# Three bank pairs for the gram products, and the inverse's room zeroed later, in an eight-group delta-rule kernel

## The reference, cut to what matters

```python
x = x + attn(cond(x, ...), ...); x = x + ffn(cond2(x, ...), ...)      # layer 0; layer 1 is like it
...
diff = jnp.where(lower, g[..., :, None] - g[..., None, :], 0.0)
decay = jnp.where(lower, jnp.exp(diff), 0.0)
A = jnp.where(strict, -(k_beta @ jnp.swapaxes(k, -1, -2)) * decay, 0.0)
attn = solve_triangular(eyeC - A, eyeC, lower=True, unit_diagonal=True)
v_c = attn @ v_beta
...
attn_i = jnp.where(lower, q_i @ jnp.swapaxes(k_i, -1, -2) * d_i, 0.0)
```

## Time and profile before

| | us |
|---|---|
| median of 3 runs | 1463.92 (1461.48 to 1468.37) |
| profiled execution, its own time | 1463.3 |
| its span, first to last instruction | 1461.5 |
| around the span | 1.8 |
| mean granted TensorE clock, share of full speed | 0.989 |
| PE busy | 1370.2 (94%) |
| DVE busy | 1074.0 (73%) |
| ACT busy | 854.9 (58%) |
| POOL busy | 461.6 (32%) |

### The profile page before, as it was taken

The page is one execution under the profiler, slowest core; times in us unless marked ns, Lnnn a source line. Parts: engine busy times, 40 slices in busy tenths (PEclk is TensorE's granted clock), DMA queues, the critical chain, the costliest instruction groups (busy, mean ns, idle before and its releaser), DMA issues.

```text
span 1461.5 us, 22073 instructions
## 1 busy us (share of the span) xinstructions
PE 1370.2 (94%) x7888; PEld 767.5 (53%) x7888; DVE 1074.0 (73%) x2468; ACT 854.9 (58%) x1745; POOL 461.6 (32%) x375
## 2 busy tenths in 40 slices
PE   0969999999999999999999999998999999999998
PEld 0534744754664574574475466475444444444443
DVE  8888889889789889888978978965589675613000
ACT  4577677668678667767766867855433433212432
POOL 5151161161153135116116115315063343200432
PEclk9989999999999999999999999989999999999999
DMA  3120030030021022003003002102283444100220
GB/s 107 49 87 16 15 123 16 2 115 23 16 76 62 17 63 75 16 16 122 11 7 111 27 16 76 33 17 93 59 238 94 124 125 119 58 0 0 74 100 29
DMA packets 39093, 88.70 MB, mean 61 GB/s; under 512 B 5385, under 2 KB 25353, under 8 KB 37841
## 3 DMA queue, kind: packets, MB, share of 16 engines
q1 hardware_dynamic: 38704, 87.23, 19.4%
q10 hardware_dynamic: 288, 0.14, 0.1%
HBM read 84.77 MB, written 2.59 MB: 60 GB/s over the span
## 4 chain that ended last, share of the span: by engine, by line
PE 77%; DVE 12%; ACT 5%; POOL 3%; issue 2%; DMA 1%; DVEq 0%; ACTq 0%; SPq 0%; POOLq 0%
PE bank L511 14%; PE bank L1799 12%; PE bank L1777 11%; PE bank L573 6%; PE bank L548 5%; PE bank L1898 5%; PE bank L610 4%; PE bank L625 4%; PE bank L540 3%; DVE conv L1070 3%; PE bank L605 2%; ACT z L886 2%; PE bank L616 2%; PE bank L627 2%; PE bank L533 2%
## 5 line engine op out<-in xcount | busy, mean ns | idle before, releaser
L1070 DVE SCALAR_TENSOR_TENSOR conv<-bank,taps,conv 128x510 f32<-128x510 f32 x366 | 270.6, 744 | 27.6 <-ACT conv L810 18.3
L511 PE MATMUL bank<-rT,wf 128*128 128x512 f32 x512 | 254.7, 612 | 1.9 <-DVE rT L238 1.2
L1649 POOL TENSOR_TENSOR ffn_weighted<-ffn_relu,ffn_wide 128x512 f32<-128x512 f32 x96 | 128.3, 1369 | 302.2 <-PE bank L1799 152.7
L1799 PE MATMUL bank<-ffn_weighted,feat 128*128 128x512 f32 x400 | 187.5, 597 | 3.9 <-POOL ffn_weighted L1649 3.9
L1777 PE MATMUL bank<-rT,feat 128*128 128x512 f32 x400 | 188.0, 597 | 0.0
L1313 POOL TENSOR_TENSOR sq<-sq,qsq 128x512 f32<-128x512 f32 x64 | 83.0, 1297 | 278.0 <-ACT sq L996 277.0
L1660 ACT ACTIVATE ffn_relu<-bank 128x512 f32<-128x512 f32 x100 | 59.6, 596 | 184.7 <-PE bank L1777 184.6
L511 PEld LDWEIGHTS bank<-rT,wf 128*128 128x128 f32 x512 | 90.3, 192 | 82.6 <-issue 73.3
L1799 PEld LDWEIGHTS bank<-ffn_weighted,feat 128*128 128x128 f32 x400 | 76.3, 191 | 100.8 <-issue 99.1
L1777 PEld LDWEIGHTS bank<-rT,feat 128*128 128x128 f32 x400 | 76.0, 191 | 93.6 <-issue 93.1
L573 PE MATMUL bank<-rT,wz 128*128 128x512 f32 x256 | 113.0, 599 | 8.4 <-DVE m L1171 7.2
(11 more groups left out here) (235 smaller groups left out, 2604.4 us busy)
## 6 DMA issues: line engine op xcount, KB each, us to landing
z<-decay_rows SPq DMA_DIRECT2D x64, 384.0 KB, 3.9
ffn_wide<-ffn_shares SPq DMA_DIRECT2D x64, 256.0 KB, 5.2
feat<-in_L_chunks_dram SPq DMA_DIRECT2D x25, 512.0 KB, 4.2
wf<-in_wf_dram SPq DMA_DIRECT2D x8, 1024.0 KB, 4.8
wz<-in_wz_dram SPq DMA_DIRECT2D x8, 512.0 KB, 3.6
wo<-in_wo_dram SPq DMA_DIRECT2D x8, 512.0 KB, 3.8
ffn_wide<-ffn_shares SPq DMA_DIRECT2D x8, 512.0 KB, 4.0
m<-in_fT_dram SPq DMA_DIRECT2D x2, 512.0 KB, 5.1
```

Source lines behind the costliest of these rows:

```text
L511: ins = pe.matmul(banks[bank_of(p, n)][:], wf[:, c, ORDER[n // NH], :], rT[:, c, halves(n % NH)], start=(c == 0), stop=(c == CT - 1))
L1070: dve.scalar_tensor_tensor(acc[:, :, k:], src[:, :, 0:T - k], taps[:, ORDER[n // NH], KS - 1 - k:KS - k], acc[:, :, k:], ALU.mult, ALU.add ...
L1649: pool.tensor_tensor(hw[:, j, u, :], h2[:, j, u, :], wide[:, j, u // NH % BLOCKS, halves(u % NH)], ALU.mult).then_inc(weighted, 1)
L1799: last = pe.matmul(banks[4 + 2 * c + h][:], chunk[:, slot, CT + t, c * P:(c + 1) * P], of, start=start, stop=stop, skip_group_check=True)
```

## The change

The gram products rotate over three pairs of banks instead of two; the third is 6 and 7. PE's waits are set anew: gram 2 waits until ACT has read the norm sums in banks 6 and 7 (in group 0 the two sums of the k norm), grams 3 to 7 wait for DVE's step n - 3 instead of n - 2, and the outputs in banks 6 and 7 wait for step 5, the last gram that used these banks. POOL zeroes `inv` and sets its diagonal behind the mask of n = 5 (the sixth) instead of ahead of that of n = 2 (the third).

```diff
+GRAM_BANKS = ((2, 3), (0, 1), (6, 7))
...
         def gram(g, n):
-            b0, b1 = (2, 3) if n % 2 == 0 else (0, 1)
+            b0, b1 = GRAM_BANKS[n % 3]
...
             for n in range(1, GK * B):
-                if n >= 2:
-                    pe.wait_ge(m_ready, g * PAIRS + 2 * n - 2)
+                if n == 2:
+                    if first:
+                        pe.wait_ge(lk_done, GK)
+                    else:
+                        pe.wait_ge(ln_done, before)
+                    gram(g, n)
+                elif n > 2:
+                    pe.wait_ge(m_ready, g * PAIRS + 2 * (n - 3) + 2)
                     gram(g, n)
...
             if not first:
-                pe.wait_ge(ln_done, before)
+                pe.wait_ge(m_ready, g * PAIRS + 12)
                 for u in (2, 3):
...
(DVE's loop over the same steps)
-                b0, b1 = (2, 3) if n % 2 == 0 else (0, 1)
+                b0, b1 = GRAM_BANKS[n % 3]
...
(POOL's group)
-            pool.memset(inv, 0.0).then_inc(inv_set, 1)
-            pool.wait_ge(inv_set, 2 * g + 1)
-            pool.sem_inc(pool_passed, 1)
-            pool.memset(inv.rearrange("p i c -> p (i c)")[:, ::SB + 1], 1.0).then_inc(inv_set, 1)
...
             for n in range(AHEAD, GK * B):
                 hide(g, n)
+                if n == AHEAD + 3:
+                    pool.memset(inv, 0.0).then_inc(inv_set, 1)
+                    pool.wait_ge(inv_set, 2 * g + 1)
+                    pool.sem_inc(pool_passed, 1)
+                    pool.memset(inv.rearrange("p i c -> p (i c)")[:, ::SB + 1], 1.0).then_inc(inv_set, 1)
                 if first:
                     add_tap(HF + n)
```

## The result

The changed kernel takes 1457.52 us (median of 17 runs, 1452.89 to 1461.37) against 1468.37 (17 runs, 1461.48 to 1471.6) for the kernel before on the same chips: ratio 0.9935, 95% interval 0.992 to 0.995. It is faster by a little more than half a per cent. The time lies 5.5 us above the 1452.0 forecast and 0.5 above the range. The profiled execution took 1459.27 us, span 1457.5, at a mean granted clock of 0.988 (before 1463.3, 1461.5, 0.989).

A forecast was written before the change was run, and what follows sets the result against it. PE was taken as the bound, held to a lead of two grams. Gains 6 x 1.84 + 0 + 0.65 = 11.7 us took the span from 1461.5 to 1449.8, 1451.6 with 1.8 around it, median near 1452; range 1445 to 1457.

The forecast's parts named there:

- 6 x 1.84: Groups 1 to 6: each gains the 1.84 us by which the inverse was ready before PE reached `below32`.
- What bounds the stage, and the banks: Gram stage: PE loses time only by leading two steps; a third bank pair starts the gates 2.15 us earlier.
- The memset's hold, s = 0: DVE's slice operations: the early mask gives 0.73 us, the memset holds the second slice, so DVE's shift s is 0.
- The cap by the inverse: At `below32`, groups 1 to 6: PE comes 2.05 us earlier, waits some 0.2 for the inverse; gain 1.84 + s.
- Group 0 and group 7: Group 0 gains 0.65 us from an earlier projection; group 7, without slack, gains only DVE's shift s, taken as 0.
- The longer hold: Slice operations: load late or small memset holds too, s = -0.4; gain 8.9 us, 1454.5; chance 0.11.
- No hold: Slice operations: the second slips past the memset, s = 0.9; gain 17.2 us, 1446; chance 0.20.
- POOL keeps its turn: Second slice operation waits until the seventh mask is done, step 3 1.4 us late; gain 1.9, 1461.5; chance 0.08.
- The gain was not given back: Rival denied here: DVE's pace, or gates and inverse, absorb PE's lead; 0 to 3 us gained, 1461; chance 0.07.
- nothing became slower: Rival denied here: both slice operations starved, step 3 starts 3 us late; 9.3 us slower, 1472.5; chance 0.03.

The follow-up runs named there:

- the banks alone: Changed kernel with the memsets put back ahead of the third mask, so only the third bank pair differs from the kernel before: 1457.49 us, ratio 0.9932.
- Memset only: Kernel before, two bank pairs and old waits, with the memsets moved behind the sixth mask: 1468.31 us, ratio 1.0009.
- memsets last: Changed kernel with the memsets behind the eighth mask instead of the sixth: 1451.94 us, ratio 0.9895 to the kernel before.
- the later inverse: One DVE operation of 1.23 us added ahead of the elimination: kernel before 1472.12 us, ratio 1.0013; changed kernel 1489.84 us, ratio 1.0116.
- the repeat: The changed kernel run and profiled again, unaltered: 1456.4 us, ratio 0.9929 to the kernel before.
- before, late inverse: Kernel before with one added DVE operation of 1.23 us ahead of the elimination, its output overwritten: 1472.12 us, ratio 1.0013.
- slices in the gap: Changed kernel, memsets behind the eighth mask and both slice operations moved ahead of DVE's block transpose: 1448.02 us, ratio 0.9866 to the kernel before.

## Why the prediction was right or wrong

**Which step failed.** Two terms of the sum were mis-sized, and the mechanisms stood in the main. The larger is its last step, "the profiled execution lies 0.6 below the median of the three runs, so the median should be near 1452": it took the level of three runs for that of the kernel, which lies 4.45 us higher. The smaller is "6 x 1.84", which measured 9.4 us and 7.7 in the two profiles. From 1468.37 the forecast would have read 1456.5.

**What bounds the stage, and the banks: right.** "PE loses time only because it may lead by two steps" was true. The gates start 2.20 us earlier against gram 1 in group 1 (predicted 2.15; 1.78 to 2.16 in the others), gram 6 has the single wait, 0.2 there and up to 0.5 in the others, and the banks alone have the whole ratio.

**The memset's hold, s = 0: right in what it does, not in its order.** I had the second slice operation at 1.3 us; it is 0.39, and the first is 1.53 to 1.96. POOL kept its turn for the memset behind the mask, DVE did not get in between (in the change repeated it did so once, in group 7, where the two take 0.84 and 1.11). Since one held operation then waits for both, step 3 starts as predicted, 8.81 to 9.24 us behind gram 1 in the first profile and 8.85 to 9.17 in the second, against 8.86. s was +0.05 to -0.4, on average -0.1 in groups 1 to 6. "Memset only" and "memsets last" show it from both sides. The rule of the Trainium skill (SBUF — State Buffer, Who interferes with whom) that VectorE in its two-port mode and GpSimd exclude each other for a whole instruction agrees with 1.53 beside the memset and 0.28 without POOL, though no trace shows in which mode the operation ran. That a GpSimd operation that only writes leaves VectorE alone holds, on that page, for operations with two SBUF inputs. The slice operations read one tensor, so these runs do not test it.

**The cap by the inverse: there, but it hardly holds PE, and "6 x 1.84 = 11.04" was too large.** The prediction had PE 0.2 us ahead of the inverse. The fifth gate costs 0.27 and not 0.1, so PE comes at almost the time of the inverse: it idles 0.02 to 0.07 us at `below32` in five of the six groups and 0.4 in group 3. Without the cap these five would gain some 0.1 each (PE takes 23.99 from the first gate to `below32`, where 23.61 and the 0.27 make 23.88). That the slack is used up is shown by the later inverse, which costs the changed kernel its full length and the kernel before nothing in groups 3 to 6. The repeat measured 1.79, 1.79, 1.13, 1.49, 1.64 and 1.56, in sum 9.4; the first profile 7.7 (1.39, 0.91, 0.29, 1.78, 1.65, 1.68). What made them smaller, each from its row:

- `below32` starts 2.13 to 2.15 us behind the start of the inverse's turn (249.60 - 247.47) and not 2.07: 0.08 in each group. The prediction had 1.97 for the turn and 0.1 behind it; they measure 1.98 to 2.01 and 0.14.
- The slack was read in group 1 and used for six. In group 3 DVE starts the elimination some 0.4 late in every kernel without the added operation, the one before included, where 0.46 and not 0.1 lies between its transpose and the first operation:
```profile
463.08 2.00 DVE L1188 STREAM_TRANSPOSE mt<-sq 128x1024 f32<-128x1024 f32 x1 [0.61 <-ACT sq L866]
465.53 0.26 DVE L1197 TENSOR_TENSOR tmp<-mt,rs 128x16 f32<-128x16 f32 x2 [0.46 <-DVE mt L1188]
```
  Its slack was 1.47. Before the change PE was later still and it cost nothing; now it is paid.
- s of -0.1 on average.
- The "issue" pauses, in which PE waits for its program: 2.1 us in the first profile, 0.2 in the repeat. The forecast had no term for them.

**Group 0 and group 7: right in size up to `below32`.** Group 0 gained 0.54 to 0.67 against 0.65; the banks alone give it (0.65), and why is not traced further. Group 7 gained nothing of its own up to `below32` in the repeat (0.04); it lost 0.4 in the first profile, and its wait there is 4.3 us instead of 2.4, as PE is earlier and the inverse is not. Behind it the repeat lost 0.86 again, with 17.1 us at the lower clock instead of 13.65, of which the forecast had nothing.

**The absolute time: the base was wrong.** 1452 was 1463.92, the median of three runs, minus 11.9. The same kernel has a median of 1468.37 over 17 runs. These 17 fall into two parts, 1461.5 to 1464.4 (7 runs) and 1467.2 to 1471.6 (10), those of the changed kernel into 1452.9 to 1455.2 and 1457.2 to 1461.4, and two of the first three came from the lower part. Of the miss of 5.5 us, 1468.37 - 1463.92 = 4.45 is this base. The other 1.1 is the gain: 10.85 between the medians (9.5 by the ratio) against 11.9.

The granted clock goes with these parts. It was 0.989 or 0.99 in the changed kernel's seven runs below 1456 us and 0.985 to 0.988 in its ten above. The 54 further runs of the kernel before, taken beside the experiments, lie between 1460.22 and 1472.54 us; times their own mean clock they lie between 1447.2 and 1453.1, and a step of 0.001 in the clock is already 1.5 us. Their medians are 1469.14, 1469.16 and 1467.72. Why the lower level lasts longer in one execution than in another stays open. Three runs were too few to stand for the kernel.

**The rivals.** "The longer hold" (8.9 us) lies nearer to the 9.5 by the ratio, the forecast's 11.9 nearer to the 10.85 between the medians. Its terms were not those that acted: its s of -0.4 was reached once, in group 7 of the first profile. "No hold" is refuted by the rows of "memset only" and of the change. "POOL keeps its turn" was right in the order and wrong in the price, since the load was early enough for mask and memset to end where the slice operations had ended before. The gain was not given back, and nothing became slower.

## What to carry to other kernels

When a faster engine runs into the next thing due, read the slack in each repetition, not in one. A pause that costs nothing before the change is paid once the slack is gone. Here the better move was to bring DVE's steps ahead, on which grams, bank 0 and the inverse all hang: two slice operations moved into a gap of DVE, and the memset behind them, brought 0.7 us per group on top of the 1.8 of the banks (119.0, 117.2, 116.48). A GpSimd operation without a deadline belongs where VectorE runs nothing that it can hold. Forecast the difference, and give the absolute time the spread of the base.

## What the runs showed of the hardware that was not expected

- A memset on POOL holds a one-input `tensor_scalar` of DVE for its whole length: 0.28 us alone, 0.63 to 1.01 when a mask was under way, mostly 1.50 to 2.01 through mask and memset (the kernels with the memset behind the sixth mask).
- A PE wait of 1.27 us ahead of a burst of small matmuls was followed by 27.3 us at a granted clock of 0.50, in groups 3 and 5 of one kernel, at a price of 12 us each. The four other groups of that kernel waited as long and kept the full clock. In group 7 every kernel has such a wait and a stretch of 13.65 us or more at the lower level. One profile of that kernel was read; its nine runs have mean granted clocks of 0.959 to 0.98. What decides it is open.
- PE pauses 0.1 to 1.3 us, mostly within bursts of small matmuls, because its instructions come late. All 19 such pauses stand at the same place of a piece of 256 instructions and end 1.2 to 1.6 us behind a 16 KB packet of the instruction queue. There was none in groups 1 to 6 where PE never waited ("slices in the gap"), while "before, late inverse" had one where PE had not waited either. Why a packet comes in time in one group and late in another is open.
- The time of an execution follows how long the lower clock level lasts in it: behind group 7's mix stage 469.9 to 476.5 us, and less half of the 3.4 to 17.1 us at 0.50 the same within 0.8 us in eleven profiles of ten kernels.
